# Small jobs and the convolution moved inside the slots of a scan kernel, with a new prologue and tail

## The reference

```
h       = x W^T + b + 2 (x A[i]) B[i]                    # cond: a low-rank pair per sample
u, gate = split(h W_in^T)                                # 2048 channels each
u       = silu(causal_conv(u, 4 taps) + conv_b)
dt, Bm, Cm = rmsnorm each of split(u Wx^T)               # 64 + 16 + 16
delta   = softplus(dt Wdt^T + dt_bias)
state   = exp(delta A) * state + (delta u) Bm            # per step; 2048 x 16 states, 256 steps
y       = (state . Cm + u D) * silu(gate)
x       = x + y W_out^T
z       = cond2(x)                                       # base weight, bias, low-rank pair
x       = x + top-2-of-8 experts (rank 64) of z, weighed by softmax of z gate^T
```

## Time and profile before

| | |
|---|---|
| median of 3 runs | 2527.34 us (2526.14 to 2530.01) |
| profiled execution, its time | 2525.12 us |
| its span, first to last instruction | 2523.3 us |
| PE, DVE, POOL, ACT busy | 2261.6, 2234.2, 2122.8, 1621.0 us |
| first L1271 (slot 0) starts | 144.17 us |
| last L1271 (slot 127) starts | 2454.65 us |

### The profile page before, as it was taken

The page is one execution under the profiler, slowest core; times in us unless marked ns, Lnnn a source line. Parts: engine busy times, 40 slices in busy tenths (PEclk is TensorE's granted clock), DMA queues, the critical chain, the costliest instruction groups (busy, mean ns, idle before and its releaser), DMA issues.

```text
span 2523.3 us, 30527 instructions
## 1 busy us (share of the span) xinstructions
PE 2261.6 (90%) x10128; PEld 1907.4 (76%) x10128; DVE 2234.2 (89%) x2104; ACT 1621.0 (64%) x3768; POOL 2122.8 (84%) x1092
## 2 busy tenths in 40 slices
PE   7988999999889998999979998899989877787878
PEld 6867877788678876788768887788767765676767
DVE  1379998999899998999989998999989999999892
ACT  1377667766677666776677666776667765775450
POOL 0089888998889988999889988899889998999880
PEclk9989999999899999999999998999999998899989
DMA  6463444444355443544445443544345322432332
GB/s 211 127 214 106 133 144 154 141 135 137 119 175 159 142 122 120 197 138 140 125 159 166 136 132 111 186 148 149 106 136 176 127 99 85 162 129 100 109 110 85
DMA packets 133114, 350.05 MB, mean 139 GB/s; under 512 B 38669, under 2 KB 43277, under 8 KB 131485
## 3 DMA queue, kind: packets, MB, share of 16 engines
q1 hardware_dynamic: 110190, 296.19, 36.6%
q10 hardware_dynamic: 22768, 51.93, 6.0%
HBM read 337.04 MB, written 11.02 MB: 138 GB/s over the span
## 4 chain that ended last, share of the span: by engine, by line
DVE 31%; PE 30%; ACT 14%; POOL 13%; issue 10%; ACTq 1%; DMA 0%; SPq 0%; DVEq 0%; POOLq 0%
DVE scan L1254 18%; ACT scan L1088 8%; POOL st L1478 7%; DVE st L1266 7%; PE ubank L614 5%; PE ubank L585 4%; POOL st L1486 4%; DVE ubank L1235 3%; PE gbank L567 3%; PE late L668 2%; PE scan L585 2%; PE late L701 2%; PE small L641 1%; ACT ubank L946 1%; PE scan L567 1%
## 5 line engine op out<-in xcount | busy, mean ns | idle before, releaser
L1478 POOL TENSOR_TENSOR st<-w_sb,bc 128x1024 f32<-128x1024 f32 x512 | 1199.2, 2358 | 150.8 <-PE gbank L631 138.1
L1254 DVE TENSOR_TENSOR_SCAN scan<-scan,st 128x1024 f32<-128x1024 f32 x512 | 1156.2, 2285 | 37.9 <-POOL st L1478 24.8
L1088 ACT ACTIVATE scan<-delta,A_sb 128x255 f32<-128x255 f32 x2048 | 846.0, 459 | 0.1
L1486 POOL TENSOR_TENSOR st<-st 128x1024 f32<-128x1024 f32 x256 | 603.6, 2358 | 53.9 <-DVE st L1266 43.2
L1085 ACT ACTIVATE scan<-iota 128x4 f32<-128x4 f32 x512 | 86.9, 170 | 671.8 <-DVE st L1266 650.5
L585 PE MATMUL ubank<-h,wt 128*128 128x256 f32 x1712 | 423.8, 404 | 94.8 <-ACT qg L1174 90.7
L614 PE MATMUL ubank<-h,wt 128*128 128x256 f32 x2048 | 476.9, 387 | 34.9 <-ACT qg L1174 29.3
L614 PEld LDWEIGHTS ubank<-h,wt 128*128 128x128 f32 x2048 | 397.6, 195 | 94.8 <-ACT qg L1174 32.7
L585 PEld LDWEIGHTS ubank<-h,wt 128*128 128x128 f32 x1712 | 346.3, 204 | 162.2 <-ACT qg L1174 110.2
L1266 DVE TENSOR_TENSOR st<-scan,bc 128x1024 f32<-128x1024 f32 x384 | 453.6, 1207 | 0.0
L668 PE MATMUL late<-yg,wt 128*128 128x256 f32 x1792 | 411.3, 389 | 39.3 <-DVE x L1291 33.2
(11 more groups left out here) (219 smaller groups left out, 2266.0 us busy)
## 6 DMA issues: line engine op xcount, KB each, us to landing
wt<-in_W_in SPq DMA_DIRECT2D x256, 512.0 KB, 3.6
wt<-in_W_out SPq DMA_DIRECT2D x128, 512.0 KB, 3.4
wt<-in_cond_W SPq DMA_DIRECT2D x64, 512.0 KB, 3.6
bc<-bc_rows ACTq DMA_DIRECT2D x64, 512.0 KB, 6.9
wt<-G_tiles SPq DMA_DIRECT2D x32, 512.0 KB, 3.7
wt<-in_ffn_B SPq DMA_DIRECT2D x20, 512.0 KB, 3.5
xb<-in_x SPq DMA_DIRECT2D x8, 1024.0 KB, 6.3
x<-in_x ACTq DMA_DIRECT2D x28, 256.0 KB, 4.0
```

The costliest lines, as they stand in the source:

```text
L1088: last = fn(t[:, k, 1:T], delta[:, c, 1:T], ACT.Exp, scale=A_sb[:, col:col + 1])
L1254: v_.tensor_tensor_scan(Tps[q % 2][:, :], Tps[q % 2][:, :], x_, 0.0, ALU.mult, ALU.add).then_inc(scan_done, 1)
L1478: tt(st[:, n % ST_RING, :, :], w_sb[:, i % 2:i % 2 + 1, :].to_broadcast([P, NQ, T]), bc[:, 0, q * NQ:(q + 1) * NQ, :], ALU.mult).then_inc( ...
L1486: tt(st[:, n % ST_RING, :, :], st[:, n % ST_RING, :, :], st[:, (n - 1) % ST_RING, :, :], ALU.add).then_inc(add_done, 1)
```

## The change

DVE runs `scan(i, 2)` before the convolution taps. PE runs `ms` ahead of the late job, `wT` behind the half job, and the end job ahead of the wait for the silus instead of behind the gate chunk. The prologue loads x first, waits for the B rows of the low-rank pair only at the first chunk's last product, preloads the exp/ln table, does `ms` and `dt` before any `cond` of sample 1, and leaves five instead of four `cond` chunks to slot 0. The part jobs of c = 13 to 15 take 1, 2 and 3 chunks more, and the tail that much less; in slot 127 DVE does y of slot 126 earlier, POOL drops its last add and fold and PE sums both planes itself; at the end the expert weights get homes of their own.

```
-            conv_tap(v, k) for u_chunks(i-1)      # DVE, slot i, behind add_first
-                if weigh: soft_max_step(b - 1, 5)
                 scan(i, 2)
+                if weigh: soft_max_step(b - 1, 5)
+            conv_tap(v, k) for u_chunks(i-1)
...
+def small_turn(i):
+    kind = small_job(i)[0] if small_job(i) else None
+    return {"ms": 0, "wT": 2}.get(kind, 1)
...
             for i in range(CHUNKS):               # PE
+                lead, turn = small_job(i), small_turn(i)
+                if lead and turn == 0: run(lead, i)
                 if late_job(i): run(late_job(i), i)
-                if small_job(i): run(small_job(i), i)
+                if lead and turn == 1: run(lead, i)
                 if i: sum_states(i - 1)
                 if half_job(i): run(half_job(i), i)
+                if lead and turn == 2: run(lead, i)
+                if end_job(i): run(end_job(i), i)
                 if i == 0:
-                    for m in range(4, KH): pro_cond(1, m)
+                    for m in range(3, KH): pro_cond(1, m)
                 ubank_free(i)
...
                 if i + 1 < CHUNKS: gate_chunk(i + 1)
-                if end_job(i): run(end_job(i), i)
                 if part_job(i): out_part(*part_job(i), i)
...
-            for t in PRO_TILES[0:2]: load_tile(t)          # SP, prologue
+            load_x(0)
             sp.wait_ge(idx_ld, 32)
-            load_cond(0)
+            rA = load_factors(0); load_tile(PRO_TILES[0]); load_rows(0, rA)
...
-            pro_cond(1, 0)                                 # PE, prologue
             mean_square(("ms", 0, 0))
-            pro_cond(1, 1)
             dt_proj(("dt", 0, 0))
             dt_proj(("dt", 0, 1))
-            pro_cond(1, 2)
-            pro_cond(1, 3)
-            gate_chunk(0)
+            pro_cond(1, 0)
+            pro_cond(1, 1)
+            gate_chunk(0)
+            pro_cond(1, 2)
...
             fn_exp_table()                                 # ACT, prologue (new)
             evac(("xp", 0, 0)); evac(("ms", 0, 0)); store_rows(0)
             evac(("dt", 0, 0)); softplus(0, 0); load_B(0, 0); load_B(0, 1)
             evac(("dt", 0, 1)); softplus(0, 1); decay(0, 0)
...
-                    cs = range(8) if part == 0 else range(8, 12)
+                    cs = 8 if part == 0 else 4 + k
...
                 add(i, 2)                                  # POOL
-                add(i, 3)
-                fold(i)
                 if i + 1 < CHUNKS:
+                    add(i, 3)
+                    fold(i)
                     dbu(i + 1, 3)
...
             expert_in(LAST, 2, ...)                        # PE, tail
             weights_t(ubank).then_inc(t_wT, 1)
+            expert_in(LAST, 3, ...)
             for m in range(EK):
-                pe.wait_ge(t_ev, KH + m + 1)
-                weights_b(m, quarter(m)[:, 0:T])
+                weights_b(m, wb_home(m))
```

More of the change, by code:

```diff
@@ L189, in slot_tiles @@
     if i == 0:
-        tiles += [("cond", 1, m) for m in range(4, KH)]
+        tiles += [("cond", 1, m) for m in range(3, KH)]
     tiles += [("u", v, 0) for v in u_chunks(i)]
@@ L193, in slot_tiles @@
         tiles += [("gate", i + 1, 0)]
-    if end_job(i):
-        tiles += job_tiles(end_job(i))
     if part_job(i):
         part, k = part_job(i)
-        tiles += [("wo1", 2 * k, 0), ("wo1", 2 * k + 1, 0)] if part == 0 else [("wo2", k, 0)]
+        tiles += [("wo1" if part == 0 else "wo2", 2 * k, 0), ("wo1" if part == 0 else "wo2", 2 * k + 1, 0)]
     return tiles
-PRO_TILES = [("cond", 0, m) for m in range(KH)] + [("u", v, 0) for v in range(NC)] + [("cond", 1, m) for m in range(4)] + [
-    ("gate", 0, 0)]
+PRO_TILES = [("cond", 0, m) for m in range(KH)] + [("u", v, 0) for v in range(NC)] + [("cond", 1, 0), ("cond", 1, 1),
+    ("gate", 0, 0), ("cond", 1, 2)]
 TAIL_TILES = [("wo3", m, 0) for m in range(PAIRS)] + [("A", LAST, m) for m in range(EK)] + [
@@ L862, in _ @@
                     run(half_job(i), i)
+                if lead and turn == 2:
+                    run(lead, i)
+                if end_job(i):
+                    run(end_job(i), i)
                 if i == 0:
-                    for m in range(4, KH):
+                    for m in range(3, KH):
                         pro_cond(1, m)
@@ L919, in _ @@
                     pe.wait_ge(t_ev, KH + 2 * EK + m - 3)
-                expert_out(LAST, m, quarter(m % 4)[:, 0:T]).then_inc(t_mm, 1)
+                n = TILE_NO[("B", LAST, m // 2)]
+                pe.wait_ge(*loaded(n))
+                for k in range(EK):
+                    if m == 0:
+                        pe.wait_ge(t_ev, KH + EK + k + 1)
+                    last = mm(quarter(m % 4)[:, 0:T], wt[:, n % W_RING, (m % 2) * EK + k, :], hw[:, k, :],
+                              start=(k == 0), stop=(k == EK - 1))
+                last.then_inc(t_mm, 1)
         @block.scalar
@@ L1423, in _ @@
                 scan(i, 3)
+                if i == CHUNKS - 1:
+                    y_sum(i - 1)
+                    y_gate(i - 1)
                 mul(i, 2)
@@ L1427, in _ @@
                 mul(i, 3)
-                if i:
+                if i and i < CHUNKS - 1:
                     if i == NC - 1:
@@ L1499, in _ @@
             delta_add(0, 0)
+            weight(0)
+            dbu(0, 0)
             delta_add(0, 1)
-            weight(0)
-            for q in range(Q):
+            for q in range(1, Q):
                 dbu(0, q)
```

154 lines of the change are left out of this document (91 added, 63 removed).

## The result

| | before | after |
|---|---|---|
| median us | 2526.74 (2525.87 to 2530.01) | 2444.76 (2442.70 to 2446.16, 4 runs) |
| profiled execution, span | 2525.12, 2523.3 | 2442.70, 2440.9 |
| first and last `add_first` (L1271, now L1320) | 144.17, 2454.65 | 128.70, 2374.02 |
| from the last one to the end of the span | 68.65 | 66.88 |

The ratio is 0.9675, with a 95% interval of 0.9661 to 0.9690: 82 us faster. The forecast was 2441.

A forecast was written before the change was run, and what follows sets the result against it. DVE was taken to bound the steady slots, PE close behind. Terms -56 - 17 - 7 - 7 - 3.6 + 4 = -86.6 took the profiled 2525.1 us to 2438.5; 2.2 more for the median gave 2441, range 2422 to 2482.

The forecast's parts named there:

- small jobs: PE's order in c = 11, 13 and 14: norm and decay waits go, -17, and y_sum waits, -7.
- the 56: DVE's waits ahead of the convolution taps go: -56 us, including 26 us in the six c = 14.
- friction: PE's late half jobs at y_sum and POOL's tight slots: 0.8 us a batch, five batches, +4.
- prologue: Before slot 0: x first, ms, norm and dt no longer waiting; most given back at slot 1; -7 together.
- part jobs and tail: c = 13 to 15 of the last batch +1.5, up to the adapter -3.3, the end -1.8: together -3.6.
- Rival 1: PE can't take the later silu; slots c = 3 to 12 keep their pitch: 27 us less gain, 2468; 15%.
- cover: decay(i+1, 0) waits for its buffer anyway, so ACT's delay in steady slots is hidden, by 0.04 us.
- rival 4: A table load holds ACT longer after a wait; decay 2.5 us late in 96 slots: +240, 2681; 1%.
- rival 3: PE loses 1.5 us in ubank_free in each convolving slot and never catches up: 2621; 5%.
- rival 2: Stalls of c = 13 and 14 only move, dt waiting in PE's list for norm: 40 us less, 2481; 7%.
- the 132 given as a sign: Expected sign in the trace: add_first (L1271) of slot 0 starts near 132 us.
- The step that slot 1 gives most of the rest back at `gate_chunk(1)`: Slot 0 starts 8 us earlier, but slot 1 waits for that gate, leaving -2.7, between +1 and -4.

The follow-up runs named there:

- Experiments 9: Changed kernel with dt behind the half job in c = 3, c = 8's cond product moved to c = 10, and the end reordered: 2451.49 us.
- experiment 10: Changed kernel with the end repaired and W_out jobs split around the cond job in c = 3, 5, 7, 8: 2448.97 us.
- experiment 12: Changed kernel with gate_chunk(1) ahead of batch 1's last three cond products, and wT evacuated ahead of the last expert product's copy: 2437.28 us.
- experiments 6: Changed kernel with one more silu of the gate, into an unused tile, ahead of the real one: 2459.56 us.
- experiment 8: Changed kernel with the convolution taps one place further on, behind scan 3: 2673.66 us.
- experiment 2: Kernel before with only PE's order changed in c = 11, 13 and 14: 2479.28 us.
- Experiment 1: Kernel before with only the convolution taps moved behind scan 2: 2502.58 us.
- experiments 11: Kernel of experiment 10 with gate_chunk(1) ahead of the last three cond products of batch 1: 2445.38 us.
- experiments 4: Kernel before with only the part jobs and the tail changed: 2525.87 us.
- experiment 5: Changed kernel with the taps put back ahead of scan 2: 2471.37 us.
- experiment 7: Changed kernel with the load of the exp table issued twice in each slot: 2443.38 us.

## Why the prediction was right, and where its terms were off

The whole was right to 4 us, and the mechanism in the steady slot to 0.06 us at the points named on ACT and PE. That the sum came so close is in part luck: its terms were off by up to 3.8 us in both directions. The runs put a price on each part:

| part | forecast | measured |
|---|---|---|
| small jobs, with the taps' wait in c = 14 | -17 - 7 - 24 = -48 | -46.4 (alone) |
| taps, the rest of the 56 less friction | -32 + 4 = -28 | -27 (in place), -23.1 (alone) |
| prologue | -7 | -9.2 |
| part jobs and tail | -3.6 | +0.2 |
| sum | -86.6 | -82.4 (the four alone: -78.5; the whole change: -82.0) |

- **The taps.** The pitch fell by 0.40 and not 0.31, for the overlap of records that a wait hides: over the some 70 slots of batches 1 to 6 that fell by it 6 us more. (Slots of 17.56 us were 6 or 7 of a batch's sixteen and not "most"; those of other lengths fell by the same 0.40.) The friction was sized too small: +4 forecast, and c = 3 and c = 8 alone are 0.93 and 0.95 us longer than the steady 17.16 on the mean, 9.4 us in five batches; c = 10, in the CAST, adds 0.47 in each, 2.3 us, by a term that the prediction didn't have. The two errors, pitch and friction, nearly cancel. I had followed PE from c = 6 on and charged 0.4 us at c = 8; c = 3, for which the prediction itself lists 19.4 us of PE's work, I left out of the walk, and I did not add up the stretch. Experiments 9 and 10 are two other orders, and both moved PE's lateness to another slot without removing it. They do not show a floor: in c = 3 to 10 PE's records add up to between 139.5 and 140.9 us in batches 1 to 5 of the changed kernel, as the stretch lasts 140.5 to 141.6, and in batch 3 of experiment 12 the same jobs in the same order took 139.25 in 139.95. In the kernel before they add up to 138.2 in a stretch of 141.7, and DVE's to 138.1. So the two engines have nearly the same work there, and PE, even so, idles some 0.6 to 0.9 us in c = 6; whether a third order would bring the stretch down is open. Rival 1 (PE can't take the later silu) holds for a part of the batch, at 1.9 us a batch. That it is the silu's lateness as such is not shown.
- **The cover** of `decay` was 0.08 us, forecast 0.04; experiments 6 and 8 show that beyond it a delay comes out in full (0.20 of 0.28, 2.11 of 2.2). The price that rival 4 named, +240 for 2.5 us past the cover, was of the right size (229 for 2.2), only its cause didn't arise: the silu stands 1.29 us behind the start of its table load. Nor did rival 3 arise: PE takes the u chunk 1.5 us later and the steady slots still fall to 17.16.
- **Small jobs.** Right, and right in place: experiment 2 shows that the 24 us at the taps of c = 14 came from PE's list, against rival 2: with only that list changed, c = 11, 13 and 14 of batches 1 to 5 give 38.5 us, and no other kind of slot there changes by more than 0.1 us in sum. Experiment 1 is the other side: the taps moved, and the stalls stayed.
- **Prologue.** Slot 0 came 15.5 us sooner (forecast 8 in words, 12 by the 132 given as a sign), slot 2 9.9 and not 7. The start gave 5.7 instead of 4.4, and the first `delta_add` came 13.4 us sooner (113.73 against 127.14), where 7 and the start's 4.4 were forecast. The step that slot 1 gives most of the rest back at `gate_chunk(1)` was right (5.5 of 9.8 us; forecast 5.3 of 8), and experiments 11 and 12 took 3 to 4 us of that away.
- **Tail.** The step that failed is "`wT` is made under the last expert product, L730 starts 1.3 us sooner": the product was, its evacuation was not, being behind a copy in ACT's list that I hadn't read for this step. L963 starts 0.1 us sooner behind the adapter, not 1.3. A second thing was not in the sum at all: PE comes to it from idling and small records, the granted clock falls to half in its first part (0.89 on the mean over its records, 1.00 before), and it takes 1.7 us longer. Together 1.6 us more behind the adapter than before, where 1.8 less was forecast. +1.5 for the part jobs and -3.3 up to the adapter were right.
- **Left out:** batch 7's first slots. POOL is busy 17.32 of 17.55 and 16.86 of 17.10 us in c = 0 and 1 of it, where before they lasted 16.3 and 16.0, and slots 0 to 2 give back 2.7 us. Experiments 1 and 2 show it in c = 1 (+0.75 and +0.84), with the tail and the prologue untouched. I read it so: DVE comes sooner there, and POOL no longer has the time that DVE's stalls left it; no run isolates this.
- **The signs.** "Wrong would be DVE waits at `y_sum` in c = 7 to 9" did occur, 0.84 to 0.91 us in c = 8, and cost what is said above; of waits on ACT at a scan, batches 1 to 5 show only 0.27 and 0.19 us, in c = 1 of batches 1 and 5.

## What to carry over

Before moving a step later in an in-order list, work out for the engine that waits for it where its next output is needed, to the hundredth: here 0.08 us of cover decided between -27 and +200 us. Add up each engine over stretches of several slots and not only over a slot or a whole batch: where two engines have nearly the same work (here 138.2 and 138.1 us over c = 3 to 10), a wait of one tends to come out at the other. When a product is moved forward, move its evacuation in the other engine's list as well.

## What the hardware showed that I had not expected

- An idle time on DVE understates what its removal gives: back-to-back records overlap by 0.08 us here, so a wait of 0.31 cost 0.39 to 0.40.
- The prologue's length varies between executions: with the same prologue the first `add_first` stood between 127.7 and 131.5 us, and in c = 3 a slot between 17.5 and 18.9 in two runs of one program. The medians of that program's two runs are 1.4 us apart.
- A busy record of DVE can be a wait: a CAST of 128x16 elements lasted 0.30 to 2.29 us, and ended within 0.05 us of a POOL instruction each of the 84 times that slots c = 10 of batches 1 to 6 show it.
- A short idle time ahead of long work cost more than itself here: with 0.73 us of it and eight small records in front, the last 64 records ran partly at half clock and took 15.75 us, with the same order in experiments 4, 5 and 7 15.77, 15.72 and 15.76; before, and in the four kernels with the end repaired, 14.08 and 13.98.
- A request for an activation table set that is loaded already left no load in the trace (129 in both runs, the request issued once or twice in a slot).
